# A chain of six transformer stages on one core: normalisation moved into the cross-attentions' last batch, weights loaded ahead, new heads of three stages

## The reference

```
h = rmsnorm(x, norm_in_w)
hc = conv(h, conv_w)                      # depthwise, 4 taps
h = silu(hc + conv_b)
q, k, v = h @ q_w, h @ k_w, h @ v_w
alpha = sigmoid(h @ alpha_w + alpha_b); beta = sigmoid(h @ beta_w + beta_b)
gate = sigmoid(silu(x @ u1_w + u1_b) @ u2_w + u2_b)
```

## Time and profile before

| | us |
|---|---|
| median of 3 runs (lowest, highest) | 2910.34 (2906.39, 2911.12) |
| profiled execution: its own time | 2914.03 |
| its span, first to last instruction | 2912.1 |
| TensorE busy | 2666.9 (92%) |
| VectorE busy | 1379.0 (47%) |
| ScalarE busy | 1069.4 (37%) |
| GpSimd busy | 481.4 (17%) |
| mean granted TensorE clock, share of full speed | 0.959 |

### The profile page before, as it was taken

How to read it: one execution, slowest core, us unless ns; L and a number is a source line. 1 busy time by engine, 2 the same in 40 slices (tenths; PEclk the granted TensorE clock), 3 DMA queues, 4 the chain that set the end, 5 groups by cost and what they waited for, 6 DMA issues and landing times. The chain is left out here.

```text
span 2912.1 us, 94584 instructions
## 1 busy us (share of the span) xinstructions
PE 2666.9 (92%) x43316; PEld 1881.4 (65%) x43316; DVE 1379.0 (47%) x2217; ACT 1069.4 (37%) x1483; POOL 481.4 (17%) x406
## 2 busy tenths in 40 slices
PE   6999999999997699989999999999868899988798
PEld 3766667666665466655666666666637777777565
DVE  3544544545436711125444545454345554545377
ACT  2333333333333321123444444444334444444322
POOL 2424333243322000000000000000001111111000
PEclk9999999999997699999999999999969999999899
DMA  2110111101100000130111111011020000000100
GB/s 87 36 36 24 42 30 31 42 24 42 30 2 13 30 29 29 43 112 24 31 42 30 42 30 42 26 41 30 3 79 3 3 3 3 3 3 4 77 1 15
DMA packets 48625, 88.90 MB, mean 31 GB/s; under 512 B 8496, under 2 KB 43120, under 8 KB 46832
## 3 DMA queue, kind: packets, MB, share of 16 engines
q1 hardware_dynamic: 48240, 82.96, 9.3%
HBM read 81.89 MB, written 1.05 MB: 28 GB/s over the span
## 5 line engine op out<-in xcount | busy, mean ns | idle before, releaser
L531 DVE TENSOR_REDUCE x_mx<-banks 128x2 f32<-128x800 f32 (+1 forms) x512 | 506.0, 991 | 215.6 <-PE banks L653 171.7
L678 PE MATMUL banks<-x_wv,x_cT 128*128 128x256 f32 (+1 forms) x1664 | 419.0, 394 | 10.9 <-DVE x_nmb L538 9.3
L600 PE MATMUL banks<-x_cT,x_wk 128*128 128x400 f32 (+1 forms) x1024 | 382.9, 516 | 17.4 <-DMA x_cT<-in_ctx 17.4
L678 PEld LDWEIGHTS banks<-x_wv,x_cT 128*128 128x128 f32 (+1 forms) x1664 | 297.6, 188 | 93.2 <-issue 36.3
L438 ACT ACTIVATE x_PT<-banks 128x1024 f32<-128x1024 f32 (+1 forms) x208 | 213.0, 1024 | 379.4 <-PE banks L710 294.0
L438 ACT ACTIVATE x_PT<-banks,x_kbs 128x1024 f32<-128x1024 f32 (+1 forms) x208 | 231.7, 1114 | 328.4 <-PE banks L710 328.4
L549 DVE COPY x_V<-banks 128x512 f32<-128x512 f32 (+1 forms) x224 | 146.2, 653 | 329.1 <-PE banks L678 328.7
L710 PE MATMUL banks<-x_qbd,x_kT 32*128 32x128 f32 x6656 | 289.2, 273 | 0.0
L600 PEld LDWEIGHTS banks<-x_cT,x_wk 128*128 128x128 f32 x1024 | 188.6, 192 | 148.0 <-issue 32.8
L696 PE MATMUL banks<-x_PT,x_V 128*32 128x64 f32 x13312 | 270.5, 222 | 2.8 <-ACT x_PT L438 2.7
L696 PEld LDWEIGHTS banks<-x_PT,x_V 128*32 128x32 f32 x13312 | 204.9, 109 | 88.4 <-issue 54.7
(11 more groups left out here) (321 smaller groups left out, 3628.7 us busy)
## 6 DMA issues: line engine op xcount, KB each, us to landing
x_cT<-in_ctx SPq DMA_DIRECT2D x96, 400.0 KB, 3.6
x_cT<-in_ctx SPq DMA_DIRECT2D x32, 401.0 KB, 3.7
e_wu<-in_mo_up SPq DMA_DIRECT2D x9, 512.0 KB, 3.7
e_wd<-in_mo_down SPq DMA_DIRECT2D x9, 512.0 KB, 4.5
x_mrow<-in_mask_row SPq DMA_DIRECT2D x1, 3202.0 KB, 11.1
t_w<-in_db_w SPq DMA_DIRECT2D x3, 1024.0 KB, 7.3
d_wqk<-in_db_qk SPq DMA_DIRECT2D x1, 2048.0 KB, 8.1
t_wgu<-in_fp_gu SPq DMA_DIRECT2D x1, 1536.0 KB, 10.2
```

The source lines that it names most:

```text
L531: dve.reduce_max(mx[:, H0[k]:H0[k] + 3:2, kb], g.PS[:, first:first + 2, 0:KBS[kb]], AXX).then_inc(max_read, 1)
L600: last = pe.matmul(PJ[pb][:, 0:KBS[k]], wk[:, c, gg, :], cT[:, (p + 1) % 2, c, KB0[k]:KB0[k] + KBS[k]], start=c == 0, stop=c == KC - 1)
L678: last = pe.matmul(PJ[pb][0:CHK[c + k], D * k:D * k + D], cT[:, p, cc, 128 * (c + k):128 * (c + k) + CHK[c + k]], wv[:, cc, :], start=cc = ...
```

## The change

- The block that loads X goes. In the first cross-attention SP issues wk, bk and the first of four blocks of context, then X and the identity, then the rest; VectorE and TensorE wait for X in front of the normalisation.
- In both cross-attentions: GpSimd casts the keys of batch 0 as soon as each block is evicted, in front of its wait for w_in. The first q wait is for 2 of the 4 evictions, and for all 4 before batch 8 (TensorE: behind the bias product). The bias product moves into step -1, behind the table product. In step -1 GpSimd makes Dxb before Dx. The mask row and mfirst count up a semaphore of their own, m_in, for which ScalarE waits in front of L421.
- The normalisation behind each cross-attention moves into it: in step 15, behind values(0), VectorE takes the moments of tiles 0 to 6; ScalarE's root follows the last oT; in step 16 VectorE writes XN of tiles 0 to 6 between the denominators and the addition to X, then does tile 7 alone; TensorE's transposes and ScalarE's copies to XNT are the block's last work.
- All latent weights, and of the delta rule's the q and k weights, u1, u1b, nw, cw and cb, are allocated ahead of the cross-attention and issued by its SP behind the last context load.
- The delta rule's head: the mean square comes from the layer normalisation's moments with three small operations; the convolution runs in four quarters of 256 columns, each followed by its two SiLUs; project(0, q and k) starts after the first quarter, and gate and beta products, with their additions and sigmoids, go between the projections; wout's scaling goes behind the sums of squares; the copy to hct goes, and the projections read hcT. Loads come in three groups: ahead (6), p_in (v and alpha weights, issued first), w_in (12).

```diff
+def ln_most_moments(dve, g, n, m):
+    s = g.sems
+    for t in range(NT - 1):
+        dve.bn_stats(g.stats[:, t, :], g.X[:, t, :]).then_inc(s["bn"], 1)
+    dve.wait_ge(s["bn"], 2 * NT * n + NT - 1)
+    for t in range(NT - 1):
+        dve.bn_aggr(g.mv[:, t, :], g.stats[:, t, :]).then_inc(s["bn"], 1)
+    dve.wait_ge(s["bn"], 2 * NT * n + 2 * (NT - 1))
+    dve.tensor_scalar(g.rs[:, 0:NT - 1], g.mv[:, 0:NT - 1, 1], 1e-5, None, ALU.add).then_inc(s["most_ve"], 1)
+def ln_most_vector(dve, g, m):
+    dve.wait_ge(s["most_sd"], m + 1)
+    dve.reciprocal(g.rs[:, 0:NT - 1], g.sd[:, 0:NT - 1]).then_inc(s["most_rs"], 1)
+    dve.wait_ge(s["most_rs"], m + 1)
+    for t in range(NT - 1):
+        dve.tensor_scalar(g.XN[:, t, :], g.X[:, t, :], g.mv[:, t, 0:1], g.rs[:, t:t + 1], ALU.subtract, ALU.mult).then_inc(s["xn"], 1)
...
 cross_attention, SP
             for k in range(NKB):
                 sp.dma_start(cT[:, 0, :, KB0[k]:KB0[k] + KBS[k]], ...).then_inc(ctx_in[0][k], 16)
+                if k == 0 and x is not None:
+                    sp.dma_start(g.X[:, :, :], x).then_inc(g.sems["x_in"], 16)
+                    sp.dma_start(g.ident[:, :], g.c["ident"]).then_inc(g.sems["x_in"], 16)
...
+            for dst, src, arrived in coming:
+                sp.dma_start(dst, src).then_inc(arrived, 16)
 GpSimd
             pool.wait_ge(set_p, 2)
+            keys(Bank(SECT[0][2]), SECT[0][1][0], 1)
             pool.wait_ge(w_in, 16 * NLOAD)
-            pool.wait_ge(q_out, 4)
+            pool.wait_ge(q_out, 2)
 ScalarE
             run(act, body)
+            ln_most_root(act, g, m)
+            ln_last_root(act, g, n + 1)
+            ln_copies(act, g, n + 1)
 VectorE
                 if attend:
                     values(0)
+                if b == B - 1:
+                    dve.wait_ge(wo_read, B // 2 - 1)
+                    ln_most_moments(dve, g, n + 1, m)
...
                 if tail and not attend:
                     denominators()
+                    ln_most_vector(dve, g, m)
                     add_output()
+                    dve.wait_ge(wo_read, B // 2)
+                    ln_last_vector(dve, g, n + 1)
 TensorE
+                    if not attend:
+                        bias_product()
...
             run(pe, body)
+            ln_tensor(pe, g, n + 1)
...
 delta_rule, VectorE
+            dve.tensor_tensor(ms[:, :], g.mv[:, :, 1], g.rs[:, :], ALU.mult).then_inc(ms_done, 1)
+            dve.tensor_tensor(rs[:, :], ms[:, :], g.rs[:, :], ALU.mult).then_inc(ms_done, 1)
+            dve.tensor_scalar(rs[:, :], rs[:, :], 1e-6, None, ALU.add).then_inc(ms_done, 1)
...
+            for k in range(4):
+                dve.wait_ge(ht_out, KC * (k + 1))
+                for tap in range(4):
+                    for c in range(KC):
+                        out = conv[:, c, 256 * k:256 * k + 256].rearrange("p (b s) -> p b s", b=4)
+                        x = conv_in[:, c, 4 * k:4 * k + 4, tap:tap + S]
+                        if tap == 0:
+                            dve.tensor_scalar(out, x, cw[:, c, 0:1], None, ALU.mult).then_inc(conv_done, 1)
+                        else:
+                            dve.wait_ge(conv_done, 8 * k + 2 * tap + c - 1)
+                            dve.scalar_tensor_tensor(out, x, cw[:, c, tap:tap + 1], out, ALU.mult, ALU.add).then_inc(conv_done, 1)
 ScalarE
+            act.wait_ge(g1_full, 2)
+            convolved(0)
+            for t in F:
+                act.activation(g1T[...], g.P[4 + t][0:RDL, :], ACT.Silu, bias=u1b[:, :]).then_inc(g1_out, 1)
...
-            projected(0, "q0", "q1", "k0")
+            convolved(1)
+            projected(0, "q0", "q1")
+            convolved(2)
+            projected(0, "k0")
             squared(0, "qq", "k0", sq[:, :, :], qn)
+            convolved(3)
             projected(0, "k1")
             squared(0, "kk", "k1", sqk[:, :, :], kn[:, :, :])
+            act.wait_ge(w_in, WIN)
             projected(0, "a0", "a1")
+            gates()
             norms(0)
 TensorE
-            project(0, *BANK)
+            project(0, "q0", "q1")
+            gate_products()
+            project(0, "k0", "k1")
+            beta_products()
+            pe.wait_ge(p_in, 16 * NPD)
+            project(0, "a0", "a1", "v0", "v1")
+            pe.wait_ge(g2_add, 4)
+            pe.wait_ge(b_add, 1)
+            pe.wait_ge(setup, 4)
+            pe.wait_ge(pool_zeroed, LV)
             levels(0, False, True)
```

More of the change, by code:

```diff
@@ L128, in xnt_ready @@
     eng.wait_ge(g.sems["xnt"], NT // 2 * (n + 1))
-def load_x(nc, g, x):
-    with nc.Block() as block:
-        @block.sync
-        def _(sp):
-            sp.dma_start(g.X[:, :, :], x).then_inc(g.sems["x_in"], 16)
-            sp.dma_start(g.ident[:, :], g.c["ident"]).then_inc(g.sems["x_in"], 16)
-            sp.wait_ge(g.sems["x_in"], 32)
 def store_x(nc, g, out):
@@ L315, in _ @@
             if mask:
-                loads += [(mT8[:, :], mask["T"]), (mrow8[:, :], mask["row"].to_broadcast([128, B * S2])),
-                          (mfirst[:, :], g.c["mfirst"])]
+                loads += [(mT8[:, :], mask["T"])]
             if rel:
@@ L322, in _ @@
                 sp.dma_start(dst, src).then_inc(w_in, 16)
+            if mask:
+                sp.dma_start(mfirst[:, :], g.c["mfirst"]).then_inc(m_in, 16)
+                sp.dma_start(mrow8[:, :], mask["row"].to_broadcast([128, B * S2])).then_inc(m_in, 16)
             for k in range(NKB):
@@ L339, in _, with scores_table, keys @@
             pool.memset(V[:, :, :, 16:17], 1.0).then_inc(set_p, 1)
+            def scores_table(b, p):
+                if later(b):
+                    pool.wait_ge(s_full, NCH * (b - 1) + 1)
+                pool.tensor_tensor(
+                    Dx[:, 1 - p, :, :].rearrange("p j (h q) -> p (j h) q", h=H),
+                    Ds[:, :, :].rearrange("p j h -> p (j h)")[:, :, None].to_broadcast([128, 2 * H, 32]),
+                    idq32[:, None, :].to_broadcast([128, 2 * H, 32]), ALU.mult).then_inc(dx_done, 1)
+            def keys(bank, plan, p):
+                for k in range(NKB):
+                    for gg in (0, 1):
+                        pb, use = plan.K[k][gg]
+                        pool.wait_ge(free[pb], bank.value(pb, use))
+                    pool.tensor_copy(kbf[:, :, KB0[k]:KB0[k] + KBS[k]], kT[:, 1 - p, :, KB0[k]:KB0[k] + KBS[k]])\
+                        .then_inc(kbf_done, 1)
             def body(bank, plan, i, p, flags):
@@ L367, in body @@
                                 idq[:, jj, None, :].to_broadcast([128, H, S]), ALU.mult).then_inc(dxb_done, 1)
[L368 to L374 removed]
+                        if not attend:
+                            scores_table(b, p)
+                    if attend:
+                        keys(bank, plan, p)
                 if attend and rel:
@@ L607, in _ @@
                 key_block(Bank(SECT[0][2]), SECT[0][1][0], -1, 1, k)
+            if x is not None:
+                pe.wait_ge(g.sems["x_in"], 32)
             ln_tensor(pe, g, n)
@@ L616, in _, with bias_product @@
                 last.then_inc(q_full, 1)
-            pe.wait_ge(bvx_done, 2 if rel else 1)
-            for j in range(4):
-                last = pe.matmul(OT[:, 0:D], bvx[:, j, :], wo[:, j, :], start=j == 0, stop=j == 3)
-            last.then_inc(bias_full, 1)
             pe.wait_ge(set_v, NSET)
             pe.wait_ge(set_p, 2)
-            pe.wait_ge(q_out, 4)
+            pe.wait_ge(q_out, 2)
+            def bias_product():
+                pe.wait_ge(bvx_done, 2 if rel else 1)
+                for j in range(4):
+                    last = pe.matmul(OT[:, 0:D], bvx[:, j, :], wo[:, j, :], start=j == 0, stop=j == 3)
+                last.then_inc(bias_full, 1)
+                pe.wait_ge(q_out, 4)
             def body(bank, plan, i, p, flags):
@@ L1447, in _, with tile @@
             pool.wait_ge(w_in, WIN)
[L1448 to L1457 removed]
+            def tile(t):
                 for l in range(LV - 1):
@@ L1471, in tile @@
                                                    ALU.add), f"XT0{f}")
-            next_tile(0)
-            for t in range(NT - 1):
-                tile(t, False)
-            tile(NT - 1, True)
+            for t in range(NT):
+                tile(t)
         @block.scalar
         def _(act):
-            ln_scalar(act, g, n)
-            act.wait_ge(w_in, WIN)
-            act.wait_ge(ms_done, 2)
+            act.wait_ge(ms_done, 3)
             act.activation(sd[:, :], rs[:, :], ACT.Sqrt).then_inc(sd_done, 1)
-            for t in F:
-                act.wait_ge(g1_full, t + 1)
-                act.activation(g1T[:, 512 * t:512 * t + 512], g.P[4 + t][0:RDL, :], ACT.Silu, bias=u1b[:, :]).then_inc(g1_out, 1)
+            act.wait_ge(a_in, 16 * NAD)
             for k in range(4):
```

275 lines of the change are left out of this document (143 added, 132 removed).

## The result

The changed kernel takes 2874.44 us (median of 4 runs, 2872.9 to 2876.29) beside 2909.95 for the kernel before (4 runs); the ratio is 0.988, 95% interval 0.9866 to 0.9893. That is 35.5 us less. The forecast was 2872 us, a gain of 38.6 us; the time lies 2.4 us above it and inside the range of 2861 to 2886.

A forecast was written before the change was run, and what follows sets the result against it. Hand-overs between stages, where TensorE idles, were taken as the bound the change touches; 8.4 + 4.3 + 6.4 + 19.5 = 38.6 us off the median 2910.34 gave 2872 us, range 2861 to 2886.

The forecast's parts named there:

- Part 1: Head of the first cross-attention: earlier key products and a shorter way to the first maximum, 8.4 us, bounds 6.4 and 12.
- the 3.7 us up to the q products: First cross-attention: key products start earlier but stall 1.9 us, so 3.7 of 5.6 us are gained.
- The 4.8 us behind the q products: First cross-attention, q products to first maximum: 5.8 us instead of 10.6, so 4.8 us go.
- Part 2: First cross-attention to latent attention: normalisation inside the last batch and weights ahead, 4.3 us, bounds 2.5 and 6.0.
- Part 3: Head of the second cross-attention: q products no longer wait for the mask row, 6.4 us, bounds 4.8 and 7.8.
- Part 4: Second cross-attention to delta rule: normalisation and loads ahead, head reordered, 19.5 us, bounds 13 and 22.
- 14.7 to the u1 products: Delta rule: u1 products start at 2117.8 instead of 2132.45, a gain of 14.7 us.
- 15.9 to the first projection: Delta rule, u1 products to first projection: 11.9 us instead of 27.8, a gain of 15.9 us.
- The loss of 10.5: Delta rule, first projection to the levels' transposes: 28.2 us instead of 17.7, as moved work now lies inside.
- Covered at nothing: Moments in the last batch, in VectorE's 4.22 us idle, and GpSimd's copy of the transposed X tile: no cost.
- The clock takes more back: Rival across all hand-overs: every gain at its lower bound, 26.7 us, time 2883.6; chance 0.17.
- The slower one: Rival in the delta rule's tiles: entered at low clock, up to 50 us longer, time 2922; chance 0.04.

The follow-up runs named there:

- the undone head: Changed kernel with the order of both cross-attentions' heads put back as before, X still behind the first weights, mask row still separate: 2885.9 us, ratio 0.9903.
- a near copy: Changed kernel with GpSimd's clearing of the levels' tiles started only after VectorE has scaled the delta rule's eight input tiles: 2880.8 us, ratio 0.9889.

## Why the prediction was right, point by point

- **What bounds the kernel** was right: the time went in the hand-overs. In the profiled pair the second cross-attention's batches moved by 0.8 us.
- **Part 1**, 7.3 for 8.4. The steps came as described. Of the 3.7 us up to the q products 2.5 came. VectorE's wait for X ended at 8.55, not 7.5 (it names ident, behind X in the same queue), so the root ended at 12.4, not 11.4; the stall of 1.67 stayed near its 1.9 only because block 0 ended late too, at 11.35 for 10.1. The 4.8 us behind the q products were 4.9, and undone, 4.9 came back. That the clock kept up behind the stall was luck of the profile: in six of nine it fell, which is the condition of the lower bound, and there the part is 4 to 6 us against the same profile of before, below its bound of 6.4.
- **Part 2**, 2.4 for 4.3, just below its bound of 2.5. From the last addition's end to the latent products it took 4.6 us, as forecast. But those products were only 4.2 us earlier than the first maximum was, where the sum had 5.7: the output product, for which no low clock had been reckoned, took 3.78 us, so the addition came 2.0 us later behind the first maximum, and not 0.5. The 1.4 us for the low clock in the latent products were 1.8 (6.65 for 4.81). The part is not a firm number, though: with the two later profiles of the changed kernel it is 1.1 and 5.1 us. So whether 4.3 was right is not shown.
- **Part 3**, 7.9 for 6.4, above its bound. Wait and q products were right (the wait 0.98, the maximum 9.6 us behind). The clock in the first pairs was taken as half real and came as whole, 3.0 us; the kernel before without the copy shows that it was not the change's. Without it the part is 4.9, and of the order in it the undone head gives 0.6.
- **Part 4**, 16.4 for 19.5. 14.7 to the u1 products were 15.8. 15.9 to the first projection were 16.2. The loss of 10.5 behind it was 12.6: the alpha products took 5.45 us at a granted clock of 0.70 where they had 3.73, and the sigmoids' table load (1.28 us, at 2130.88), which had lain beside the beta products (2152.80 before), now stands in front of the alpha sigmoids. The prediction counted two table loads on this path; there are three. Then 3.0 more were lost in the levels of tile 0. This is the mis-sized step: the sum ended at the levels' transposes, with 0.6 us for gaps, and the clock behind a wait of 3.3 us was seen, but only as the start of the rival in which tile after tile is slow. It fell once, for 3 us, and rose again. To tile 0's first GpSimd operation, reordering the head is worth 0.0 us where I had 5.4 (15.9 - 10.5). On the side of the changed kernel this part is firm: its three profiles have 60.2 us from the last addition to that point. On the other side there is one profile, with 76.6, and the kernel before without the copy has 75.0.
- **Covered at nothing**, the moments and the copy: right.
- **Slips in the sums.** Table load and two SiLUs were put at 1.6 us and take 2.2 (2107.60 to 2109.81), and 8.4 less 1.8 is 6.6 for the lower bound of part 1, not 6.4. Neither moves the forecast by more than 0.6 us.
- **Rivals.** "The clock takes more back" was right in kind for parts 2 and 4, and too strong in sum. The slower one did not come; the tiles ran at 1.00.

The terms measured, with the pieces left out that come from single profiles (3.0 of part 3, the batches, the tiles), sum to 7.3 + 2.4 + 4.9 + 16.4 = 31 us; the ratios and medians of three sets say 33.5 to 35.5, each with some 5 us to either side. The difference of 3 is smaller than the spread of part 2 alone, and stays open. Parts 1, 2 and 4 fell short of the forecast by 1.1, 1.9 and 3.1 us, and part 3 without its 3.0 by 1.5; that the total came as near as 35.5 for 38.6 is in part luck.

## What to carry to other kernels

Where the work and the loads of a hand-over wait side by side, moving only one shows the other: here 5.0 and 8.8 us alone, 15.8 together. A reordering has to be summed to the first point behind it at full clock, not to its own last instruction; the longer wait it leaves can cost what it gained. And one profile says nothing of a 7 us difference in a loop of 470 us, nor of 2 us at the end of 840: profile the same program again before explaining it. What came out alike in all three profiles of the changed kernel (55.4 to 55.5 us in the delta rule's head, 4.7 us between the last addition and the u1 products) can be built on.

## What the runs showed of the hardware

Eight scalings of 128x256 on VectorE (one tensor read) took 5.45 us beside GpSimd's clearing of 128x1024 tiles and 2.19 without it, while six taps of the convolution that read two tensors took 2.44 us, 1.9 of them beside it, and 2.46 without. The Trainium skill (SBUF — State Buffer, "SBUF: two separate sides") has the two engines share a pair of ports of which one holds the whole; the trace agrees as far as that. The table load took 1.28 us in every row, and where ScalarE had nothing else to wait for, the next ACTIVATE followed within 0.02 us, so part 4 loses nothing to the 2.7 us that were weighed there. The tile loop of one program took 469.1, 469.3 and 477.6 us with the same instructions, and 477.0 in a near copy at the same clock as the first; no row shows why.
